# A graph layer's edge sort: one-hots of four edge columns at a time, with the column innermost, read by TensorE with a step of four

## The reference

```python
src, dst                      # 20000 edges, int32, in 0..1249
deg = segment_sum(ones, dst)  # with self loops
h = xn @ W
agg = segment_sum(h[src] * dinv[src] * dinv[dst], dst)
x = x + relu(agg + b) + mixer(xn)
x = x + memory(layernorm(x))
```

## Time and profile before

| what | value |
|---|---|
| median of three runs | 900.23 us |
| profiled execution | 899.98 us |
| its span in the trace | 897.7 us |
| mean granted TensorE clock | 0.983 of full speed |
| PE busy | 818.5 us, 91% |
| DVE busy | 618.5 us, 69% |
| POOL busy | 338.8 us, 38% |
| ACT busy | 311.9 us, 35% |

### The profile page before, as it was taken

One profiled execution on the slowest core, in us unless ns is written; L12 is line 12 of the kernel. 1 busy time (PEld: TensorE's weight loads), 2 busy tenths in 40 slices (PEclk: granted clock), 3 DMA queues, 4 the chain that ended last, 5 costly groups with the idle time before them and its releaser, 6 DMA issues.

```text
span 897.7 us, 24280 instructions
## 1 busy us (share of the span) xinstructions
PE 818.5 (91%) x10394; PEld 552.7 (62%) x10394; DVE 618.5 (69%) x1306; ACT 311.9 (35%) x548; POOL 338.8 (38%) x300
## 2 busy tenths in 40 slices
PE   2999999999999989998999978998899989997898
PEld 1454444445566548763444357888889989897443
DVE  7999999976888556328633647766667757673385
ACT  1231112210222120023545525454545555554352
POOL 5221100000111040001760358776677776762560
PEclk9999999999999989999899989999999999999999
DMA  8500000030000042000085744454534444421462
GB/s 247 183 0 1 0 2 1 17 76 23 2 1 2 2 171 87 1 1 0 6 309 199 264 129 115 115 138 117 137 114 139 123 132 123 130 70 44 111 187 68
DMA packets 74961, 80.49 MB, mean 90 GB/s; under 512 B 34452, under 2 KB 57670, under 8 KB 74853
## 3 DMA queue, kind: packets, MB, share of 16 engines
q1 hardware_dynamic: 69733, 57.78, 23.0%
q0 software_dynamic: 5120, 21.14, 6.6%
HBM read 54.44 MB, written 24.39 MB: 88 GB/s over the span
## 4 chain that ended last, share of the span: by engine, by line
PE 67%; DVE 23%; issue 4%; DMA 2%; ACT 2%; POOL 1%; SPq 1%; DVEq 0%; POOLq 0%
PE bank L772 10%; PE bank L841 10%; PE bank L867 5%; PE bank L1042 4%; PE bank L582 4%; DVE rows L1541 4%; PE bank L568 4%; DVE rows L1543 3%; PE bank L788 3%; DVE rows L1670 3%; PE bank L930 2%; PE bank L789 2%; PE bank L858 2%; PE bank L943 2%; PE bank L967 2%
## 5 line engine op out<-in xcount | busy, mean ns | idle before, releaser
L772 PE MATMUL bank<-W,xT 128*128 128x512 f32 x272 | 123.8, 608 | 4.8 <-ACT big L1119 4.8
L772 PEld LDWEIGHTS bank<-W,xT 128*128 128x128 f32 x272 | 51.6, 194 | 64.5 <-issue 57.9
L546 PE MATMUL bank<-W,xT 128*125 128x512 f32 x160 | 77.8, 600 | 0.0
L1361 POOL TENSOR_TENSOR cnt_r<-cnt_r,ident_sb 125x125 fp32r<-125x125 f32 x10 | 11.4, 1142 | 173.8 <-ACT cnt_r L1107 173.8
L568 PEld LDWEIGHTS bank<-rows 128*126 128x126 f16 x360 | 43.5, 135 | 34.7 <-issue 24.2
L1676 DVE TENSOR_SCALAR rows<-iota_sb,tC 128x625 f16<-128x625 f16 x180 | 56.2, 379 | 10.5 <-PE bank L568 10.5
L568 PE MATMUL bank<-rows 128*126 128x313 f16 x360 | 58.9, 299 | 4.2 <-DVE rows L1676 4.1
L1541 DVE TENSOR_SCALAR rows<-iota_sb,gbp 125x180 f16<-125x180 f16 x160 | 56.8, 355 | 0.0
L1543 DVE TENSOR_SCALAR rows<-iota_sb,gbp 125x180 f16<-125x180 f16 x160 | 51.0, 318 | 0.0
L841 PE MATMUL bank<-big 64*64 64x64 f32 (+1 forms) x1280 | 44.3, 214 | 4.0 <-issue 3.2
L556 PE MATMUL bank<-rows 125*128 125x360 f16 x160 | 42.5, 319 | 5.1 <-DVE rows L1543 3.5
(11 more groups left out here) (337 smaller groups left out, 1975.8 us busy)
## 6 DMA issues: line engine op xcount, KB each, us to landing
big<-qkv_slots SPq DMA_DIRECT2D x40, 256.0 KB, 3.6
rows<-step_rows SPq DMA_DIRECT2D x40, 128.0 KB, 3.2
rows<-gam_rows SPq DMA_DIRECT2D x40, 128.0 KB, 3.4
big<-qkv_slots SPq DMA_DIRECT2D x80, 64.0 KB, 2.9
big<-qkv_slots SPq DMA_DIRECT2D x40, 128.0 KB, 2.9
o_slots<-big SPq DMA_DIRECT2D x40, 128.0 KB, 2.9
x_all<-in_x SPq DMA_DIRECT2D x10, 224.0 KB
out<-tC SPq DMA_DIRECT2D x10, 224.0 KB
```

Source lines behind the costliest of these rows:

```text
L546: last = mm(dst, xT[:, k, t * P:(t + 1) * P], W[:, w, k, :], start=(k == 0), stop=(k == KC - 1 and bias is None))
L772: last = mm(bank[:, b0, :], xT[:, k, t * P:t * P + 128], W[:, w, k, :], start=(k == 0), stop=(k == KC - 1))
```

## The change

`sort_four` makes three instructions of its nine. All operands become half precision, and the four edge columns become the innermost dimension, four neighbouring elements, of every operand:

- `iota4` (written once, by ACT, into a free tile of `hs`) is the row 0..179 with each number four times in a row: 720 elements.
- `e_place` and `e_ends` are half-precision copies of places and columns, and of sources and destinations, written once by DVE into `bet` and `bdec`, which are free then.
- `in_col` is the 180 x 4 one-hot of the sorted column; `oh_place` the 128 x 4 one-hot of the place; `oh_edge` is `in_col` times the two ends: 2 x 180 x 4.
- PE reads one edge column u out of `oh_place[..., u]` and `oh_edge[..., u]`, so with a step of four elements, both as stationary and as moving operand. It now waits for the whole group of four.

```diff
+        oh_place = rowsf[0:P, 0:SR * SB * 128].rearrange("p (w n u) -> p w n u", w=SR, u=SB)
+        oh_edge = rowsf[0:P, SR * SB * 128:SR * SB * (128 + 2 * SW)].rearrange("p (w a n u) -> p w a n u", w=SR, a=2, u=SB)
+        in_col = [hs[:, w, 0:SB * SW // 2].bitcast(f16).rearrange("p (n u) -> p n u", u=SB) for w in range(2)]
+        iota4 = hs[:, 2, 0:SB * SW // 2].bitcast(f16).rearrange("p (n u) -> p n u", u=SB)
...
+        e_place, e_ends = (t[0:P, :, :].rearrange("p c j -> p (c j)").bitcast(f16).rearrange("p (a j) -> p a j", a=2) for t in (bet, bdec))
...
             def sort_step(i):
-                pe.wait_ge(S["sort_oh"], i + 1)
-                mm(bank[:, 7, 0:2 * SW], oh_row[:, i // SB % SR, i % SB, :], oh_col[:, i % (SR * SB), :, :].rearrange("p a n -> p (a n)"), start=False, stop=True,
+                w, u = i // SB % SR, i % SB
+                pe.wait_ge(S["sort_oh"], i // SB * SB + SB)
+                mm(bank[:, 7, 0:2 * SW], oh_place[:, w, :, u], oh_edge[:, w, :, :, u].rearrange("p a n -> p (a n)"), start=False, stop=True,
                    skip_group_check=True).then_inc(S["sort_used"], 1)
...
             copy_tiles(0, LB, 0)
+            act.wait_ge(S["iota_loaded"], 32)
+            A(iota4, bc(iota[0:P, 0:SW], SB), ACT.Copy)
...
             def sort_four(m):
+                edges = slice(SB * m, SB * m + SB)
+                step(V.tensor_tensor(in_col[m % 2], iota4, bm(e_place[:, 1, edges], SW), ALU.is_equal))
                 if m >= SR:
                     dve.wait_ge(S["sort_used"], SB * (m - SR + 1))
-                V.tensor_tensor(oh_row[:, m % SR, :, :], bm(iota[0:P, 0:128], SB), bc(e_row[:, SB * m:SB * m + SB], 128), ALU.is_equal)
-                for i in range(SB * m, SB * m + SB):
-                    V.tensor_scalar(oh_col[:, i % (SR * SB), 0, :], iota[0:P, 0:SW], e_col[:, i:i + 1],
-                                    e_src[:, i:i + 1], ALU.is_equal, ALU.mult)
-                    V.tensor_scalar(oh_col[:, i % (SR * SB), 1, :], iota[0:P, 0:SW], e_col[:, i:i + 1],
-                                    e_dst[:, i:i + 1], ALU.is_equal, ALU.mult).then_inc(S["sort_oh"], 1)
+                V.tensor_tensor(oh_place[:, m % SR, :, :], iota4[:, 0:128, :], bm(e_place[:, 0, edges], 128), ALU.is_equal)
+                V.tensor_tensor(oh_edge[:, m % SR, :, :, :], in_col[m % 2].unsqueeze(1).broadcast_to([P, 2, SW, SB]),
+                                e_ends[:, :, edges].unsqueeze(2).broadcast_to([P, 2, SW, SB]), ALU.mult).then_inc(S["sort_oh"], SB)
...
             dve.wait_ge(S["round_step"], ROUND_STEPS)
+            step(V.tensor_copy(e_place, e_all[:, 0:2, :]))
+            step(V.tensor_copy(e_ends, e_all[:, 2:4, :]))
```

## The result

The changed kernel took 922.82 us (four runs, 921.88 to 924.27), and the kernel before 901.57 us (four runs, 900.04 to 902.94). The ratio is 1.0249, interval 1.0216 to 1.0282. The forecast was 896.4 us and its range ended at 905: sign and range were both wrong. The measured time is nearest to rival 1, whose price was 918.7.

A forecast was written before the change was run, and what follows sets the result against it. PE bounds the kernel, held up by DVE's sort one-hots: gains 4.0 + 0.6 + 0.9 = 5.5 us, losses 1.6 + 0.2 = 1.8, net 3.7 off 899.98, so 896.4 us; own range 893.7 to 897.8, 8-in-10 range ending at 905.

The forecast's parts named there:

- rival 1: Sort matmuls: PE reads a stepped operand at half rate, 0.30 us per sort; +18.5 us, 918.7 us; chance 0.14.
- PE's reads: Sort matmuls' stepped operands: no change from 0.154 us taken; the high end was half rate, 0.27 up to 0.30.
- VectorE's prices: New sort group's three DVE instructions: 0.53, 0.42 and 0.90 us, 1.73 us per group instead of 2.49.
- rival 2: Sort one-hots: DVE doesn't get two elements per cycle, a group takes 3.12 us; +25, about 925 us; chance 0.05.
- The tile on PE if nothing holds it: Projection tile with its sort matmuls, PE never waiting for DVE: 10.44 us against 11.5 now.
- The POOL collision: POOL's key-tile addition beside the group behind `keep_keys`: 1.20 us of it waited for again by DVE's second instruction.
- The gain: PE's waits for DVE's one-hots: 4.0 us in tiles 6 to 9, 0.6 in query unit 0, 0.9 in last units; 5.5 us.
- The start: PE's first sort, waiting for a whole group of four: 1.6 us later than 68.48, at some 70.1.
- the copy on ACT: ACT's 720-element copy ahead of the first exponential, waiting for `b_q` (landing at 25.3 to 25.8): costs nothing.
- The condition (1.6 us): ACT's copy would begin to cost time if the `b_q` DMA came 1.6 us later than expected.
- The clock: Tile 5 after PE's idle time, at 1.2 GHz: costs 1.4 us now, 0.2 us more after the change.
- The gain should last: Behind the sort, work is on PE alone or moves with it, so the net 3.7 us should reach the end.

The follow-up runs named there:

- experiments 1 and 2: Two standalone probe kernels, sets of 24 matmuls with operands read at various steps and runs; 360 half-precision columns took 0.153 us at step 1, about 0.32 at step 4.
- experiment 3: Changed kernel, but PE reads 360 neighbouring elements as moving operand (wrong sums), stationary step kept; 896.94 us against 898.51 before the change, ratio 0.9990.
- experiment 4: Against the kernel before, only the place one-hot (stationary) made column-innermost, moving operand as before, ACT's copy behind key tile 2; 892.44 us against 898.51, ratio 0.9919.
- experiment 6: Changed kernel with two edge columns innermost in the moving one-hots (step of two), ACT's copies behind key tile 2; 900.0 us against 901.19 before, ratio 0.9995.
- the longer gap of 8: VectorE's idle at the count-round branch; step-of-two kernel with 4, 12, 28 or 240 one-element copies added: 3.83, 3.83, 3.96, 3.81 us, against 1.5 before the change.

## Why the prediction was wrong

- **The step that failed** is *PE's reads*: "I take no change: the row nearest to the new matmul is the old one". The right value was the high end that the same paragraph had worked out, half rate: 0.318 beside 0.154. The old row has the same columns, type and partitions, and differs in the one thing that changed, so it could not be evidence about it. Between two bounds 24 us apart over 160 matmuls, nothing in the trace chose; a chance of 0.14 for rival 1 was too little. What stands in its place: the moving operand costs 1.76 ns per 16-byte stretch that it touches, 180 stretches here, 0.317 us and not 0.154 (experiments 1 and 2), and without the step the loss is gone (experiment 3).
- Beside that row, the two hits per line (the Trainium skill's Advanced Engine Details and Errata, section SBUF Cachelines) were the only thing that spoke for full rate at a distance of 8 bytes. Experiments 1 and 2 refute them for this operand.
- **Rival 1's price** was short by 4 us: 0.146 per sort and not 0.166 (3.2 us), and the start (0.8 us). A tile was to take 12.8 and took 13.1. It was built on 0.30 for 360 columns, the rate per column at half clock; what limits is another thing, with 0.317. That the two lie so close is luck: a step of eight costs 0.633.
- **VectorE's prices** were right to 0.01 us, and rival 2 (no two elements per cycle) is out. The tile on PE if nothing holds it was right too (10.44; experiments 3 and 4: 10.46). The POOL collision was priced too high: from start to start the second instruction takes 70.09 - 68.80 = 1.29, and I had added up 0.34 + 1.20 = 1.54.
- **The gain**: 5.5 us of stalls. In the changed kernel a slower PE hides them all (6.8). In experiment 4 they show as time, 5.2 us at the first count; in 3, 4.5 (its start is 1.5 us late, its lead 3.0), or 5.7 with the 1.2 us that the lower clock takes more there.
- **The start** was to be 1.6 us late. In experiment 3 it was 1.5, in the changed kernel's profile 2.56: the copy on ACT "costs nothing" held in the one and cost 1.2 in the other, since the transfer it waits for landed 2.9 to 3.4 us later than I had expected. 2.7 of them are a later issue (16.47, not 13.78) and 0.7 the transfer. The condition (1.6 us) was named in the prediction; but the "median" of the earlier trace rows is that of one transfer, and its issue time one execution's, which says nothing of how far either can move. The two casts took 0.73 (forecast 0.75); the rest, 0.64, is mostly the whole group.
- **The clock** was to cost tile 5 1.6 us. In the changed kernel it loses 13.65 - (13.12 - 0.86) = 1.4, as before; in experiment 3's profile 2.6.
- **"The gain should last"** was unsafe. With the three-instruction group, 3.0 us of lead at the first count were given back by the end of the aggregation (experiment 6); the longer gap of 8 and what follows it in the same stretch is where they go.

## What to carry to other kernels

A layout that makes the producer faster must be priced at each reader's port as well, and a row of the old layout is no price for the new one: where 160 matmuls hang on it, a probe of 24 decides in one run. In half precision, give a moving operand at least four columns in each 16 bytes that it touches (a step of two at most); put the stepped layout on the stationary operand, whose load has room beside its neighbour's matmul. And ask for the smallest innermost run that already gives the producer its rate: two did, where four was built.

## What the runs showed of the hardware

- TensorE's moving operand in half precision costs 1.76 ns per 16-byte stretch touched, or its time per column (0.42 ns at 2.4 GHz, 0.83 at 1.2), whichever is more: steps of 2, 3, 4, 6, 8 and 16 take 0.159, 0.240, 0.319, 0.477, 0.633 and 0.647 us for 360 columns. The price of a stretch is the same at both clocks: at a granted 0.50 a step of four takes 0.32 and a step of six 0.477. So at 1.2 GHz a step of four costs next to nothing over the unstepped 0.30.
- Weight loads of 128 columns go from 96 to 113 ns with a step of four, all hidden here.
- VectorE's product of half-precision operands takes 0.90 us for 1440 elements and 0.52 for 720, with an innermost run of four or of two; 512 elements take 0.43 us alone and 1.37 beside POOL's addition.
- At the same untaken branch VectorE idled 1.5 us in three kernels and 3.8 to 4.0 in nine; an instruction transfer begins inside the gap in those nine alone.
